# The router's logits of a mixture of experts: token tiles or router weights as the array's stationary side

## The chip, the cores and the metric

The kernel runs on one core of one Trainium2 chip. The metric is the device time of one execution in microseconds (us). The program is a transformer of four blocks; the change touches only the last one, the mixture of experts, which takes the last 275 us or so of the span.

## The reference, cut to what matters

There are 4096 tokens of width 256. The last block takes the layer-normalised stream `x` and computes

```python
scores = jax.nn.sigmoid(x @ gate_W) * route_scale            # gate_W: 256 x 8, eight experts
topk_scores, topk_idx = jax.lax.top_k(scores, 2)
topk_w = topk_scores / topk_scores.sum(-1, keepdims=True)
gate_full = jnp.einsum('bsk,bske->bse', topk_w, onehot)      # onehot of topk_idx
h = jax.nn.gelu(jnp.einsum('bsd,edh->bseh', x, W1) + b1, approximate=False)
y = jnp.einsum('bseh,ehd->bsed', h, W2) + b2
expert_out = jnp.einsum('bse,bsed->bsd', gate_full, y)
shared = jax.nn.gelu(x @ Ws1 + bs1, approximate=False) @ Ws2 + bs2
return expert_out + shared
```

and the stream gets the layer norm of the result added. All arithmetic is in float32. The hidden width is 128.

## The kernel before, in words

`phase_experts` works on 8 supertiles `i` of 512 tokens (`NT` = 4 tiles of 128). Per supertile there are 9 steps `k`: step 0 is the shared expert, steps 1 to 8 are the experts. The running number is `c = 9i + k`. Each engine has its own program; they meet at semaphores, and each engine works strictly in the order that is written.

- **TensorE**, step `k`: `hidden(i, k)` (six matmuls of 512 columns, L1651, for the three products of high and low parts), then inserted work for the next supertile, then `outputs(c - 3)` (twelve matmuls of 256 columns, L1670; four more, L1665, for the biases at `k` = 0). The inserted work in supertiles 1 to 6 is: at `k` = 0 the eight transposes `turn_in(i + 1)` (L172) of the normalised tokens into `psT` and `psG`; at `k` = 2 `logits(i + 1)` (L1631); at `k` = 6 `turn_gates(i + 1)` (L1638, four transposes). In supertile 0 these stand at `k` = 3, 5 and 8. `psG` is one PSUM bank: it is used for half of the turned tokens, then for the logits, then for the turned gates.
- **`logits`** before: for each of 4 token tiles and 2 halves of the width, the 128 x 128 turned tokens are the stationary side and the router's 128 x 8 weights move. A plain float32 matmul shows in the trace as two pairs of weight load and matmul, so the 8 of them are 16 pairs. The result has tokens in the partitions and 4 x 8 columns.
- **ScalarE**, step `k`: `gelu(i, k)` (L1741), then `high(c - 1)` (L1752, the rounded high part of the gated hidden values), then at `k` = 3 `sigmoid(i + 1)` (L1724, with a table load ahead of it and another ahead of the next gelu), at `k` = 4 `shift_x` (L1757), at `k` = 7 `take_gates(i + 1)` (L1732 and L1733). `take_turned` copies stand at `k` = 0. In supertile 0 the sigmoid stands at `k` = 5.
- **VectorE**, step `k` of 1 to 8: `gate(i, k)` (L1541: hidden values times the gate broadcast; the first waits for the DMA of the gates), at `k` = 2 `take_y` and the statistics of the supertile before, at `k` = 3 `route_tokens(i + 1)` (L1501 to L1525: 24 small instructions in a chain), at `k` = 4 the statistics of supertile `i + 2` (L134 to L141), at `k` = 5 `add_y` (L1565), at `k` = 6 `normalize_x(i + 2)` (L148). In supertile 0 the routing stands at `k` = 5.
- **GpSimd**, step `k`: `low(c)` (L1801, the low part, h minus its high part), and the inverse roots of the layer norms (L161).
- **SyncE** issues the DMAs. `gates_out` writes the 8 rows of gates to memory and reads them back spread over all partitions (`gb`, 2 MB).

The work for the next supertile's gates thus runs: `turn_in`, `take_turned`, `logits`, `sigmoid`, `route_tokens`, `turn_gates`, `take_gates`, `gates_out`, and then the first `gate` of the next supertile.

Column tiles occur elsewhere in this kernel: attention's products with the values (L1008) put a 128 x 32 weight block into each of four column tiles, and 256 columns move.

Of the kernel before, what the change touches and what calls it, by code (L numbers as in the profile page):

```python
# [17 lines left out]
ACT = mybir.ActivationFunctionType  # L18
AX = mybir.AxisListType

P = 128
# [1336 lines left out]
def phase_experts(nc, x, gate_w, w1, b1_cols, w2, b2, ws1, bs1_col, ws2, bs2, route_scale, ident_d, gate_rows, x_out):  # L1358
# [8 lines left out]
    with ExitStack() as ctx:  # L1367
# [3 lines left out]
        wg = m.sb("wg", [P, KD, NE])  # L1371
# [19 lines left out]
        sig, score, pick, sel1, sel2 = (m.sb(s, [P, NT, NE]) for s in ("sig", "score", "pick", "sel1", "sel2"))  # L1391
# [8 lines left out]
        psX = (psT, psG)  # L1400
        ident_in, const_in, w_in, x_in = m.sem("ident_in"), m.sem("const_in"), m.sems("w_in", 2), m.sems("x_in", 4)
# [3 lines left out]
        logits_done, sig_ready, route, gates_ready = m.sem("logits_done"), m.sem("sig_ready"), m.sem("route"), m.sem("gates_ready")  # L1405
        g_turned, gT_ready, g_out, gb_in = m.sem("g_turned"), m.sem("gT_ready"), m.sem("g_out"), m.sems("gb_in", 2)
# [12 lines left out]
        def _(sp):  # L1419
# [23 lines left out]
            sp.dma_start(wg[:, :, :], gate_w.rearrange("(k p) e -> p k e", p=P)).then_inc(const_in, 16)  # L1443
# [24 lines left out]
        def _(dve):  # L1468
# [29 lines left out]
            def route_tokens(i):  # L1498
                r.start(i)
                dve.wait_ge(sig_ready, i + 1)  # L1500
                nc.vector.tensor_scalar(score[:, :, :], sig[:, :, :], r_scale[:, 0:1], None,  # L1501
# [72 lines left out]

            nc.vector.memset(b_e[:, :], 0.0).then_inc(b_set, 1)
# [17 lines left out]
            for i in range(NST):  # L1593
                if 0 < i < NST - 1:
                    take_turned(i + 1)
                for k in range(1, E):
# [6 lines left out]
                    if k == (5 if i == 0 else 3) and i + 1 < NST:  # L1603
                        route_tokens(i + 1)
# [11 lines left out]
        def _(pe):  # L1616
# [10 lines left out]
            def logits(i):  # L1627
                pe.wait_ge(xlo_ready, KD * (i + 1))
                for n in range(NT):
                    for k in range(KD):  # L1630
                        mm = pe.matmul(psG[:, n * NE:(n + 1) * NE], xT[:, k, n * P:(n + 1) * P], wg[:, k, :],  # L1631
                                       start=(k == 0), stop=(k == KD - 1))
                mm.then_inc(logits_done, 1)

# [45 lines left out]
            for k in range(3):  # L1680
                hidden(0, k)
            turn_gates(0)

            for i in range(NST):
                for k in range(E):
# [3 lines left out]
                    if i + 1 < NST:  # L1689
# [9 lines left out]
                        if k == (8 if i == 0 else 6):  # L1699
                            turn_gates(i + 1)  # L1700
# [8 lines left out]
        def _(act):  # L1709
# [10 lines left out]
            def sigmoid(i):  # L1720
                act.wait_ge(logits_done, i + 1)
                if i:
                    act.wait_ge(gates_ready, i)
                nc.scalar.activation(sig[:, :, :], psG[:, 0:NT * NE].rearrange("p (n e) -> p n e", e=NE),  # L1724
                                     ACT.Sigmoid).then_inc(sig_ready, 1)
# [1104 lines left out]
```

## Time and profile before

| | us |
|---|---|
| time, median of 3 runs (lowest, highest) | 2087.64 (2087.29, 2089.38) |
| the profiled execution's own time | 2088.27 |
| its span | 2086.1 |
| TensorE matmul busy in the span | 1990.2 (95%) |
| VectorE busy | 1513.8 (73%) |
| ScalarE busy | 1288.2 (62%) |
| GpSimd busy | 599.2 (29%) |

All times in the profile count from the span's start. The experts' block begins at about 1812 us. Of an engine, "busy" is the time in which it executes an instruction; matmuls overlap, so that the duration of one is longer than the distance from one to the next. The numbers behind `x` count instructions.

### The profile page before, as it was taken

The numbers are of one execution on the slowest core, as the hardware profiler recorded it, in microseconds if no ns is written. First come the engines' busy times: TensorE is split into PE (matmuls) and PEld (weight loads), VectorE is DVE, ScalarE is ACT, GpSimd is POOL, SyncE is SP. The second block draws the span as 40 slices with busy tenths as digits, with TensorE's granted clock in tenths as the row PEclk, the third lists the DMA queues.
The fourth block names the chain that finished last, engine by engine and source line by source line (L and its number), as shares of the span: only waits on it lengthen the run. The fifth ranks groups of instructions, "written<-read, shape, count | busy, mean of one in ns | idle before, by whom it ended". The sixth has DMA issues, their size and how long they took to land. (4 is left out here: it accounts for less than half of the span.)

```text
span 2086.1 us, 42106 instructions
## 1 busy us (share of the span) xinstructions
PE 1990.2 (95%) x16914; PEld 1405.2 (67%) x16914; DVE 1513.8 (73%) x2466; ACT 1288.2 (62%) x2560; POOL 599.2 (29%) x480
## 2 busy tenths in 40 slices
PE   7999999999999998997999999999999999489997
PEld 6743333333333347986888888888888888478996
DVE  7889999999999976895546464646464644468774
ACT  3258888888888876785454545454545454256663
POOL 1200000000000014554334343434343433125554
PEclk9979999999999999999999999999999999789999
DMA  6832232223223222316222122212122212232221
GB/s 231 249 59 66 54 85 61 64 69 70 71 53 84 66 76 67 128 41 173 72 63 92 63 92 63 92 63 92 63 92 63 92 63 82 62 120 77 107 112 71
DMA packets 103490, 180.66 MB, mean 87 GB/s; under 512 B 24232, under 2 KB 65856, under 8 KB 98176
## 3 DMA queue, kind: packets, MB, share of 16 engines
q1 hardware_dynamic: 103296, 177.97, 28.4%
q8 instruction: 134, 2.20, 0.5%
q14 instruction: 60, 0.49, 0.1%
HBM read 138.48 MB, written 38.67 MB: 85 GB/s over the span
## 5 line engine op out<-in xcount | busy, mean ns | idle before, releaser
L741 DVE TENSOR_REDUCE att_sb_mx<-att_ps_psM 128x1 f32<-128x1024 f32 x512 | 624.6, 1221 | 27.6 <-PE att_ps_psM L978 23.8
L1192 ACT ACTIVATE att_sb_pt<-att_ps_psSO 128x512 f32<-128x512 f32 x1024 | 557.1, 597 | 95.2 <-PE att_ps_psSO L996 41.1
L978 PE MATMUL att_ps_psM<-stack_sb_k,stack_sb_q 48*128 48x512 f32 x1024 | 382.3, 454 | 4.6 <-DVE att_sb_mx L741 2.3
L996 PE MATMUL att_ps_psSO<-stack_sb_q,stack_sb_k 50*128 50x512 f32 x1024 | 373.3, 444 | 0.9 <-DMA stack_sb_q<-att_sb_mrow 0.9
L1008 PE MATMUL att_ps_psSO<-att_sb_pt,stack_sb_v 128*32 128x256 f32 x4096 | 326.4, 391 | 8.6 <-ACT att_sb_osb L1185 8.6
L996 PEld LDWEIGHTS att_ps_psSO<-stack_sb_q,stack_sb_k 50*128 50x128 f32 x1024 | 153.2, 185 | 202.8 <-ACT att_sb_pt L1192 155.5
L1008 PEld LDWEIGHTS att_ps_psSO<-att_sb_pt,stack_sb_v 128*32 128x32 f32 x4096 | 82.0, 108 | 192.1 <-issue 102.9
L2310 ACT ACTIVATE glag_sb_sg<-att_ps_psM 128x512 f32<-128x512 f32 x64 | 38.3, 599 | 250.9 <-PE att_ps_psM L2070 250.8
L2535 DVE TENSOR_TENSOR glaj_sb_dm<-att_ps_psSO,glaj_sb_dm 128x512 f32<-128x512 f32 x128 | 82.2, 684 | 133.5 <-PE att_ps_psSO L2190 133.5
L978 PEld LDWEIGHTS att_ps_psM<-stack_sb_k,stack_sb_q 48*128 48x128 f32 x1024 | 156.9, 189 | 19.3 <-DVE att_sb_mx L741 16.4
L2672 POOL TENSOR_TENSOR glaj_sb_dm<-glaj_sb_dm,glaa_sb_masked 128x1024 f32<-128x1024 f32 x64 | 156.5, 2466 | 19.0 <-DMA glaj_sb_dm<-decay_rows 19.0
L2327 ACT ACTIVATE glaj_sb_dm<-glaj_sb_dm,glaa_sb_neg_g 128x128 f32<-128x128 f32 x512 | 156.3, 391 | 0.2
L1801 POOL TENSOR_TENSOR moe_sb_hlo<-moe_sb_h,moe_sb_hhi 128x512 fp32r<-128x512 f32 x72 | 94.9, 1330 | 101.6 <-ACT moe_sb_hhi L1752 101.6
L2107 PE MATMUL att_ps_psM<-glao_sb_wo,glai_sb_yT 128*128 128x256 f32 x512 | 117.5, 382 | 0.9 <-DVE glai_sb_yT L2550 0.9
L1278 POOL TENSOR_TENSOR att_sb_mparts<-att_sb_mx,att_sb_zero 128x16 fp32r<-128x16 f32 x32 | 7.0, 220 | 383.8 <-DVE att_sb_mx L741 383.8
L1287 POOL TENSOR_TENSOR att_sb_on<-att_sb_osb,att_sb_rb 128x512 f32<-128x512 f32 x32 | 41.0, 1282 | 221.9 <-DMA att_sb_rb<-sums 221.9
L2107 PEld LDWEIGHTS att_ps_psM<-glao_sb_wo,glai_sb_yT 128*128 128x128 f32 x512 | 94.8, 190 | 13.8 <-DVE glai_sb_yT L2550 1.1
L2460 DVE SCALAR_TENSOR_TENSOR glah_sb_kg<-glag_sb_sg,att_ps_psM 128x512 f32<-128x512 f32 x64 | 44.0, 688 | 80.0 <-PE att_ps_psM L2070 65.7
L2680 POOL TENSOR_TENSOR glah_sb_kg<-glah_sb_kg,glaa_sb_to_end 128x1024 f32<-128x1024 f32 x32 | 65.0, 2032 | 92.5 <-PE att_ps_psM L2141 92.5
L1670 PE MATMUL moe_ps_psY<-moe_sb_wb_hi,moe_sb_hhi 128*128 128x256 f32 x288 | 83.7, 291 | 2.7 <-POOL moe_sb_hlo L1801 2.7
L2699 POOL TENSOR_TENSOR glah_sb_state<-glah_sb_state,glai_sb_eg 128x512 f32<-128x512 f32 x32 | 34.0, 1063 | 181.2 <-PE att_ps_psSO L2205 181.2
L2588 DVE TENSOR_REDUCE glaa_sb_osum<-glai_sb_osq 128x128 f32<-128x1024 f32 x32 | 63.7, 1990 | 30.3 <-ACT glai_sb_osq L2390 30.1
(305 smaller groups left out, 4829.0 us busy)
## 6 DMA issues: line engine op xcount, KB each, us to landing
glaj_sb_dm<-decay_rows SPq DMA_DIRECT2D x32, 1024.0 KB, 5.2
qk_parts<-stack_sb_part SPq DMA_DIRECT2D x32, 512.0 KB, 3.3
glai_sb_eg<-decay_exp SPq DMA_DIRECT2D x64, 256.0 KB, 6.3
moe_sb_gb<-gate_rows SPq DMA_DIRECT2D x8, 2048.0 KB, 7.7
stack_sb_q<-qk_parts SPq DMA_DIRECT2D x192, 64.0 KB, 3.0
stack_sb_k<-qk_parts SPq DMA_DIRECT2D x96, 128.0 KB, 4.3
att_sb_rb<-sums SPq DMA_DIRECT2D x32, 256.0 KB
attended<-att_sb_on SPq DMA_DIRECT2D x32, 256.0 KB, 4.9
```

What stands on the lines that cost most here:

```text
L741: nc.vector.tensor_reduce(mx[:, qh, 8 * r + c:8 * r + c + 1], psM[:, t % 2, :], AX.X, ALU.max).then_inc(maxima_taken, 1)
L978: mm = pe.matmul(psM[:, t % 2, c * ST:(c + 1) * ST], q[rs, g, qh, j, n * P:(n + 1) * P], k[rs, g, j, c * ST:(c + 1) * ST], start=True, sto ...
L996: pe.matmul(psS[:, ring_slot(pos), :], k[rs, g, j, s * P:(s + 1) * P], q[rs, g, qh, j, :], start=True, stop=True).then_inc(ring_done, 1)
L1008: mm = pe.matmul(psO[VW * j:VW * (j + 1), cols], v[:, KT * b + s, h:h + VW], pt[:, s % (LAG + 2), j, cols], start=(s == 0 and part == 0), ...
L1192: nc.scalar.activation(pt[:, s % (LAG + 2), ORDER[i], :], psS[:, (pos + 1) % 3, :], ACT.Exp, scale=AD ** -0.5).then_inc(ring_taken, 1)
L1670: mm = pe.matmul(psY[:, i % 2, n, :], v[:, c % 4, cols], w[:, e, :], start=False, stop=(k == E - 1 and p == 2), skip_group_check=True)
L1801: nc.gpsimd.tensor_tensor(hlo[:, c % 4, :], h[:, c % 4, :], hhi[:, c % 4, :], ALU.subtract).then_inc(hlo_ready, 1)
L2107: pe.matmul(psW[:, 0:D], yT[:, j, :], wo[:, j, :], start=(j == 0), stop=(j == J - 1))
L2327: done = nc.scalar.activation(dm[n % 2][:, h, :], dm[n % 2][:, h, :], ACT.Exp, bias=neg_g[:, u, n, h:h + 1])
L2535: nc.vector.tensor_tensor(dm[n % 2][:, hs, :], psA[:, odd, :, :], dm[n % 2][:, hs, :], ALU.mult).then_inc(ad_ready, 1)
L2672: nc.gpsimd.tensor_tensor(dm[n % 2][:, hs, :], dm[n % 2][:, hs, :], masked[:, :].rearrange("p (h t) -> p h t", h=1).to_broadcast([P, 8, P] ...
L2680: nc.gpsimd.tensor_tensor(kg[:, n % 2, :].rearrange("p (h d) -> p h d", d=GD), kg[:, n % 2, :].rearrange("p (h d) -> p h d", d=GD), to_end ...
```

## The change

The stationary and the moving side of the logits change places. The router's weights, padded from 8 to 32 columns with zeros, are the stationary side, and the 128 tokens of a tile move. The result of token tile `n` goes to partitions `32n` to `32n + 32` (a column tile of the array each), 128 columns wide: experts in the partitions, tokens in the columns. ScalarE takes the sigmoid of the whole 128 x 128 block into `sigT`; TensorE turns `sigT` back (`turn_scores`) into the second quarter of `psG`, and `route_tokens` reads the scores from there. `wg` is set to zero by VectorE before its DMA, and SyncE waits for that.

The positions move too: on VectorE `route_tokens(i + 1)` goes from step 3 to step 4 (5 to 6 in supertile 0), behind `gate(i, 4)`; on TensorE `turn_scores(i + 1)` stands at step 4 (6 in supertile 0) and `turn_gates(i + 1)` goes from step 6 to step 7 (it stays at 8 in supertile 0). In the prologue, `turn_scores(0)` follows `hidden(0, 0)`.

```diff
-        wg = m.sb("wg", [P, KD, NE])
+        wg, sigT = m.sb("wg", [P, KD, 32]), m.sb("sigT", [P, P])
...
+        psSig = psG[:, P:2 * P].rearrange("p (n e) -> p n e", e=32)
...
-            sp.dma_start(wg[:, :, :], gate_w.rearrange("(k p) e -> p k e", p=P)).then_inc(const_in, 16)
+            sp.wait_ge(wg_clear, 1)
+            sp.dma_start(wg[:, :, 0:NE], gate_w.rearrange("(k p) e -> p k e", p=P)).then_inc(const_in, 16)
...
             def route_tokens(i):
-                dve.wait_ge(sig_ready, i + 1)
-                nc.vector.tensor_scalar(score[:, :, :], sig[:, :, :], r_scale[:, 0:1], None,
+                dve.wait_ge(sig_turned, i + 1)
+                nc.vector.tensor_scalar(score[:, :, :], psSig[:, :, 0:NE], r_scale[:, 0:1], None,
...
+            nc.vector.memset(wg[:, :, :], 0.0).then_inc(wg_clear, 1)
...
-                    if k == (5 if i == 0 else 3) and i + 1 < NST:
+                    if k == (6 if i == 0 else 4) and i + 1 < NST:
                         route_tokens(i + 1)
...
             def logits(i):
                 pe.wait_ge(xlo_ready, KD * (i + 1))
-                for n in range(NT):
-                    for k in range(KD):
-                        mm = pe.matmul(psG[:, n * NE:(n + 1) * NE], xT[:, k, n * P:(n + 1) * P], wg[:, k, :],
+                for k in range(KD):
+                    for n in range(NT):
+                        mm = pe.matmul(psG[32 * n:32 * (n + 1), 0:P], wg[:, k, :], xT[:, k, n * P:(n + 1) * P],
                                        start=(k == 0), stop=(k == KD - 1))
                 mm.then_inc(logits_done, 1)
+
+            def turn_scores(i):
+                pe.wait_ge(sig_ready, i + 1)
+                pe.transpose(psG[:, P:2 * P], sigT[:, :], ident[:, :]).then_inc(sig_turned, 1)
...
-            for k in range(3):
+            hidden(0, 0)
+            turn_scores(0)
+            for k in (1, 2):
                 hidden(0, k)
...
-                        if k == (8 if i == 0 else 6):
+                        if k == (6 if i == 0 else 4):
+                            turn_scores(i + 1)
+                        if k == (8 if i == 0 else 7):
                             turn_gates(i + 1)
...
             def sigmoid(i):
                 act.wait_ge(logits_done, i + 1)
                 if i:
-                    act.wait_ge(gates_ready, i)
-                nc.scalar.activation(sig[:, :, :], psG[:, 0:NT * NE].rearrange("p (n e) -> p n e", e=NE),
-                                     ACT.Sigmoid).then_inc(sig_ready, 1)
+                    act.wait_ge(sig_turned, i)
+                nc.scalar.activation(sigT[:, :], psG[:, 0:P], ACT.Sigmoid).then_inc(sig_ready, 1)
```

## Rows read from the trace of the kernel before

**Rows 1.** Busy us (and count) per engine by window, TensorE clock, DMA share, GB/s.
```profile
1877.09:1907.85 30.76, 29.43 (x196) 26.37 (x195) 23.27 (x64) 18.88 (x32) 15.28 (x13) 1.00 0.28 105
...
1907.85:1936.98 29.13, 29.13 (x197) 26.47 (x195) 21.21 (x62) 17.73 (x30) 14.33 (x12) 1.00 0.29 110
...
sum 148.22, PE 146.04 PEld 132.24 DVE 110.93 ACT 92.31 POOL 74.52; mean PE 29.21 PEld 26.45 DVE 22.19 ACT 18.46 POOL 14.90
```

**Rows 2.** Waits of TensorE in 1800 to 2087: us in total, times, longest.
```profile
PE moe_ps_psG L1638 <- DVE moe_sb_gparts L1525: 1.6, 3, 0.8
```

**Rows 3.** The chain of waits: start, us, what.
```profile
1825.98 3.56 PE moe_ps_psG L1631 x16
...
1903.40 1.39 PE moe_ps_psH L1651 x6
...
1904.79 1.69 PE moe_ps_psG L1631 x16
...
1927.95 8.27 DMA moe_sb_gb<-gate_rows
```

**Rows 4.** Timeline of TensorE in attention: start, us, instruction, count.
```profile
400.95 0.39 PE L978 MATMUL att_ps_psM<-stack_sb_k,stack_sb_q 48*128 48x512 f32 x1
...
401.27 0.64 PE L1008 MATMUL att_ps_psSO<-att_sb_pt,stack_sb_v 128*32 128x256 f32 x8
...
401.84 0.28 PE L1016 MATMUL att_ps_psSO<-att_sb_ident,att_sb_mparts 128*32 128x128 f32 x1
```

**Rows 5.** Timeline of TensorE in supertile 2 of the experts.
```profile
1927.24 0.60 PE L172 MATMUL moe_ps_psT<-moe_sb_ident,moe_sb_xn 128*128 128x128 f32 x4
...
1928.03 0.36 PE L1670 MATMUL moe_ps_psY<-moe_sb_wb_hi,moe_sb_hhi 128*128 128x256 f32 x1
```

**Rows 6.** Timeline of ScalarE in supertile 2, and one line's durations (min/median/max).
```profile
1909.45 0.69 ACT L1741 ACTIVATE moe_sb_h<-moe_ps_psH,moe_sb_b_h 128x512 f32<-128x512 f32 x1 [2.19 <-PE moe_ps_psH L1651]
...
1910.66 1.28 ACT L1724 ACT_TABLE_LOAD   x1
...
1911.96 0.20 ACT L1724 ACTIVATE moe_sb_sig<-moe_ps_psG 128x32 f32<-128x32 f32 x1
...
1913.47 0.69 ACT L1741 ACTIVATE moe_sb_h<-moe_ps_psH,moe_sb_b_h 128x512 f32<-128x512 f32 x1
...
L2327 ACT ACTIVATE glaj_sb_dm<-glaj_sb_dm,glaa_sb_neg_g x512: 384/391/414, 976.6 to 1780.1; 128x128 f32<-128x128 f32 x171
```

**Rows 7.** Timeline of VectorE in supertile 2.
```profile
1911.31 0.68 DVE L1541 TENSOR_TENSOR moe_sb_h<-moe_sb_h,moe_sb_gb 128x512 f32<-128x512 f32 x1
...
1912.19 0.24 DVE L1501 TENSOR_SCALAR moe_sb_score<-moe_sb_sig,moe_sb_r_scale 128x32 f32<-128x32 f32 x1 [0.19 <-ACT moe_sb_sig L1724]
...
1913.36 1.11 DVE L1495 TENSOR_TENSOR moe_sb_sel<-moe_sb_pick,moe_sb_rank 128x32 f32<-128x32 f32 x1
...
1918.15 0.68 DVE L1541 TENSOR_TENSOR moe_sb_h<-moe_sb_h,moe_sb_gb 128x512 f32<-128x512 f32 x1
...
1920.81 0.68 DVE L1541 TENSOR_TENSOR moe_sb_h<-moe_sb_h,moe_sb_gb 128x512 f32<-128x512 f32 x1
...
1924.03 0.68 DVE L1541 TENSOR_TENSOR moe_sb_h<-moe_sb_h,moe_sb_gb 128x512 f32<-128x512 f32 x1
...
1924.64 2.35 DVE L148 TENSOR_SCALAR moe_sb_xn<-moe_sb_xin,moe_sb_mv,moe_sb_rs 128x256 f32<-128x256 f32 x4
```

**Rows 8.** Timeline of GpSimd in supertile 2.
```profile
1913.12 1.29 POOL L1801 TENSOR_TENSOR moe_sb_hlo<-moe_sb_h,moe_sb_hhi 128x512 fp32r<-128x512 f32 x1
```

**Rows 9.** Timeline of supertile 0: ScalarE, VectorE, TensorE.
```profile
1857.76 0.69 ACT L1741 ACTIVATE moe_sb_h<-moe_ps_psH,moe_sb_b_h 128x512 f32<-128x512 f32 x1
...
1862.38 0.68 DVE L1541 TENSOR_TENSOR moe_sb_h<-moe_sb_h,moe_sb_gb 128x512 f32<-128x512 f32 x1
...
1862.80 0.60 PE L1638 MATMUL moe_ps_psG<-moe_sb_ident,moe_sb_gparts 128*104 128x128 f32 x4
...
1867.72 0.66 PE L172 MATMUL moe_ps_psG<-moe_sb_ident,moe_sb_xn 128*128 128x128 f32 x4 [1.07 <-ACT moe_sb_gT L1733]
```

More of the change, by code:

```diff
@@ L1390, in phase_experts @@
         y, xo = m.sb("y", [P, NT, D]), m.sb("xo", [P, 2, NT, D])
-        sig, score, pick, sel1, sel2 = (m.sb(s, [P, NT, NE]) for s in ("sig", "score", "pick", "sel1", "sel2"))
+        score, pick, sel1, sel2 = (m.sb(s, [P, NT, NE]) for s in ("score", "pick", "sel1", "sel2"))
         gates, gT = m.sb("gates", [P, NT, NE]), m.sb("gT", [NE, 2, ST])
@@ L1405, in phase_experts @@
         logits_done, sig_ready, route, gates_ready = m.sem("logits_done"), m.sem("sig_ready"), m.sem("route"), m.sem("gates_ready")
+        sig_turned, wg_clear = m.sem("sig_turned"), m.sem("wg_clear")
         g_turned, gT_ready, g_out, gb_in = m.sem("g_turned"), m.sem("gT_ready"), m.sem("g_out"), m.sems("gb_in", 2)
```

## The prediction, made before the changed kernel was run

> **What bounds the kernel now.** I read the busy time by window first, one window from the third `hidden` step of a supertile to that of the next (the start of `hidden(i, 3)`, which I call P; in supertile 2 P is 1907.85, where the second window shown begins [rows 1]). The reader is to see that TensorE has 29.13 us of work in a window of 29.13 us, at the full clock, 146.04 of 148.22 us over five windows, while VectorE has 22.19 and ScalarE 18.46 on average [rows 1]. So TensorE sets the pace. The waits come next: what little TensorE waits for in the steady part is mostly VectorE's gate parts, 3 times and 1.6 us in all [rows 2]. VectorE's chain is therefore only just early enough. The chain of waits shows the same: it goes over the logits in one supertile and over the 8.27 us DMA of the gates in the next [rows 3]. The timelines last: I measure every event of supertile 2 from P and ask how much room each has.
>
> **The logits.** Removed: 16 pairs in 1.69 us, once in each of supertiles 0 to 6, and once in the prologue, in 3.56 us [rows 3]. Added: 8 float32 matmuls with 32 stationary and 128 moving columns. The nearest rows are attention's: four such matmuls of 256 columns, 8 records, take 0.57 us from their start at 401.27 to the next instruction at 401.84, and the first starts 0.32 us behind the 512-column matmul ahead of it [rows 4], where such a matmul takes 0.23 us in a row of its kind (1.39 us for six [rows 3]). So the four tiles run beside each other, two passes of 256 columns cost 0.48 us, and entering and leaving the column tiles costs some 0.09 us each. Here there are two k halves of two passes, each of 128 columns: four rounds of about 0.12 us, plus 0.2 us, 0.7 us. Bounds: 0.5 us (four rounds of 0.11 us and free changes of mode) and 1.9 us (16 passes of 0.11 us that don't overlap, with both changes). I take 0.7, since [rows 4] show the same weight shape and the same rotation over four tiles.
>
> The Trainium skill has a rule against column tiles, in the page TensorEngine Tiling (Array Packing), section Tiling Modes: changing the mode drains the array. By the trace that drain is the 0.09 us on either side, so it is in the sum; nothing else hangs on the rule.
>
> **Turning the scores back.** One transpose. Eight transposes fill 1927.24 to 1928.03 [rows 5], 0.10 us each; I take 0.13, between 0.10 and 0.30 for one that is alone. TensorE's own work per supertile falls by 1.69 - 0.70 - 0.13 = 0.86 us, to 28.3 us. Does it wait for the sigmoid? The sigmoid ends at P + 4.31 (1912.16) before [rows 6]. `hidden(4)` starts at P + 3.31 and is through at P + 4.70. A sigmoid of 128 x 128 instead of 128 x 32 takes 0.20 us at the least and 0.39 at the most, the 128 x 128 activation of line 2327 [rows 6]; I take 0.28, from the line between 0.20 us for 32 columns and 0.69 for 512. It ends at P + 4.4, 0.3 us ahead of need. No wait.
>
> **Routing behind gate 4.** This is the costly part. Before: gate 3 ran at P + 3.46, and VectorE then routed from P + 4.34 to P + 10.30, while ScalarE loaded the gelu table and did gelu 4. Gate 4 came at P + 10.30, then statistics, gate 5 at P + 12.96, gate 6 at P + 16.18 and the normalised tokens from P + 16.79 to P + 19.14 [rows 7]. TensorE turned those at P + 19.39 [rows 5]: 0.25 us of room. After: gate 4 stands ahead of the routing, and gate 4 needs gelu 4, which ScalarE ends at P + 6.31 (1914.16) since two table loads of 1.28 us lie around the sigmoid [rows 6]; with the longer sigmoid P + 6.4. So VectorE stands idle for about 1.2 us and starts to route at P + 7.05, not P + 4.34. The 24 instructions take 5.96 us of which two were stretched to about 1 us by GpSimd's `low` (the selection at 1913.36 took 1.11 us and ended with the `low` that began at 1913.12 [rows 7, 8]); without such a stretch they take 4.4. In the new place `low(3)` and `low(4)` fall on them, so I keep 5.95. They end at P + 13.0. Gate 4 is no longer behind them, so statistics follow, gate 5 starts at P + 15.0 (2.1 us later than before), and the tokens are ready at P + 21.2. From the turn to the next P TensorE took 29.13 - 19.39 = 9.74 us, now 8.75. The period is 21.25 + 8.75 = 30.0 us. It was 29.13. TensorE's 0.86 us turn into waits, at `outputs(5)` first and then at the transposes.
>
> Bounds of the routing's length: 4.4 us (GpSimd never beside it) and 6.9 us (three `low` beside it). In every other supertile the gates' DMA takes 8.3 us instead of about 7 and the statistics of y come later, so that `low(2)`, `low(3)` and `low(4)` all lie on the routing: I add 0.7 us there, a period of 30.7 us. The SBUF - State Buffer page of the Trainium skill, section Who interferes with whom, says that a VectorE instruction with two SBUF inputs and a GpSimd instruction that reads SBUF lock each other out. By that rule the stretch goes wherever `low` goes and changes no number here.
>
> **Turning the gates at step 7.** The gate parts are ready at P + 13.0, and TensorE comes there at P + 13.4; before both were at P + 10.4. No wait, and `take_gates` (ScalarE, step 7) waits for `high(6)` behind gate 6 as before. The gates' DMA keeps 0.8 us of room: gate 6 at P + 18.2, then 12.3 us to the landing (gate 6 at 1924.03, landing 1936.3, from the 8.27 us DMA issued at 1927.95 [rows 3, 7]), P + 30.5; two gates, y and its statistics and gate 3 take 5.1 us, P + 35.6, and gelu 4 of the next supertile comes at 36.4 or later.
>
> **Supertile 0 and the prologue.** Logits in the prologue save some 2 us of 3.56 [rows 3], but the scores wait for `hidden(0, 0)`, at half clock, and VectorE routes 1.5 us later: the two about cancel (bounds -1 and +1.5). In supertile 0 gate 6 moves ahead of the routing and waits for gelu 6, which starts at 1857.76 [rows 9]; routing runs from 1859.1 to 1864.9, not to 1862.47, and TensorE, which turned gates at 1862.80 without a wait, stands 2.1 us. VectorE then wins back one stretch: the turned gates reach ScalarE 0.95 us late, and TensorE's second half of the turned tokens, at 1867.72 before, comes 1 us late, which the faster logits of supertile 1 give back. P of supertile 2 is unchanged at 1907.85.
>
> **The small edits.** The memset of `wg`, some 0.1 us, runs when VectorE has nothing to do before its first tokens land, and SyncE reaches its wait four DMAs later: 0 (0.1 if it isn't covered).
>
> **The sum.** From P of supertile 2 to P of supertile 6 it was 148.22 - 30.76 = 117.46 us (the first window is 30.76) [rows 1]. After: 30.0 + 30.7 + 30.0 + 30.7 = 121.4, +3.9. In supertile 6 gate 5 comes 2.1 us later against P, and `add_y` behind it has one `low` fewer on it, -1.0: gate 6, and with it the last DMA of gates, is 5.0 us late. Supertile 7 hangs on that DMA (VectorE waits for it, then TensorE), so the end is 5.0 us late. The profiled execution took 2088.27 (span 2086.1 and 2.2 around it): 2093.2. That one lies 0.6 above the median of the runs, so I predict 2092.6 against 2087.64: slower by 0.24%.
>
> **The rivals.**
> (A) TensorE stays the bound. The routing meets only one or no `low` in its new place: 4.4 us, tokens ready at P + 19.7, then the period is 28.5 and for each of the six supertiles 0.8 us are won, one or two in the prologue lost: 2083. For it: TensorE is full in [rows 1]. Against it: `low(3)` follows gelu 4 by 0.6 us, so at least it lies at the routing's start; the change needs both `low` away.
> (B) Half of that: one stretch gone, or the 0.25 us of room larger than it seems; a period of 29.2 to 29.5, the same as before: 2086 to 2089.
> (C) The column tiles don't overlap for 128 columns, or their weight loads can't be hidden: logits of 1.7 to 1.9 us. 1.1 us more in each of five periods: 2098. This is also the case where the change doesn't do what it says. Against it: eight column-tile records in 0.57 us [rows 4].
> (D) The forecast's mechanism with routing slower still (three stretches everywhere): 2095.
>
> **How the numbers follow.** The forecast's own case has 0.50, with a range of 2090 to 2096; B 0.22; A 0.14; C 0.07; D 0.07. A measurement of this kernel tells about 0.2% (4.2 us) from nothing, so the bounds are 2083.5 and 2091.8. The forecast lies close to the upper one: a quarter of its chance falls below. Faster is A, 0.14; same is B and 0.12 of the forecast, 0.34; slower the rest, 0.52. The range reaches down to most of B and a part of A, up to C: 2084.5 to 2098.
>
> **What the changed profile would show.** The logits in 0.6 to 0.8 us (right) or over 1.5 (C). VectorE idle ahead of gate 4, released by gelu 4, about 1 us in supertiles 2, 4 and 6; the routing from P + 7. TensorE waiting for the normalised tokens at line 172 and for `low` at the outputs, 1 to 2 us in each supertile, where it waited for neither. In supertile 0 a wait of 2 us for the gate parts. If those waits are absent and TensorE is full in windows of 28.3 us, the forecast is wrong and A holds; if the waits stand there and the sum is smaller, the routing's length is the term that is off.

## The result, and the profile after

The changed kernel took 2094.73 us (median of 10 runs, 2092.85 to 2099.82), the kernel before 2087.47 (10 runs, 2086.65 to 2090.52): a ratio of 1.0035, 95% interval 1.0026 to 1.0043. It is slower by some 7 us; the forecast was slower by 5. The profiled execution of the changed kernel has a span of 2095.2 us, 9.1 more than before. 1.0 of that lies ahead of the experts' block, where nothing was changed (the block began at 1812.48 us and now at 1813.49), and 8.1 in the block, which took 273.64 us and now 281.69. The block's start lies anywhere from 1811.8 to 1817.0 us in the profiles of this page, though nothing ahead of it differs, so I compare the length of the block from here on.

The windows of the changed kernel, from the third `hidden` step of a supertile (P) to the next, columns as in [rows 1]:

```profile
1878.93:1911.12 32.19, 29.11 (x197) 24.70 (x196) 23.35 (x64) 18.43 (x31) 15.21 (x12) 1.00 0.30 109
1911.12:1941.06 29.94, 28.52 (x197) 24.89 (x196) 21.04 (x62) 18.43 (x31) 15.14 (x12) 1.00 0.28 106
1941.06:1972.29 31.23, 28.91 (x197) 24.72 (x196) 23.44 (x64) 18.43 (x31) 15.21 (x12) 1.00 0.27 103
...
sum 153.67, PE 143.82 PEld 124.12 DVE 111.63 ACT 92.21 POOL 75.70; mean PE 28.76 PEld 24.82 DVE 22.33 ACT 18.44 POOL 15.14
```

TensorE is busy for 2.2 us less in the five windows (143.82 for 146.04), and the windows are 5.5 us longer (153.67 for 148.22 [rows 1]). (Some 4.5 us of work were taken from it in them, as shown below; the matmuls beside a wait are spread, which hides a part of that.) It is no longer the engine that is full. The waits of TensorE from 1800 us to the end (total, times, longest), in the changed kernel, to be held against [rows 2]:

```profile
PE moe_ps_psY L1679 <- POOL moe_sb_hlo L1813: 11.1, 9, 1.7
...
PE moe_ps_psG L1647 <- DVE moe_sb_gparts L1529: 2.2, 2, 2.0
...
PE moe_ps_psG L1642 <- ACT moe_sb_sigT L1737: 0.8, 1, 0.8
```

The kernel before has the first of them too, but small:

```profile
PE moe_ps_psY L1670 <- POOL moe_sb_hlo L1801: 2.7, 3, 1.1
```

Those three waits lie in supertiles 0, 1 and 7. Now there is one of 1.3 to 1.4 us in each of supertiles 1 to 5: TensorE stands at the output matmuls for GpSimd's `low`, which is late because the gate ahead of it is. The two other lines are the gate parts, nearly all of it in supertile 0, and one wait of the turn-back for the sigmoid. VectorE's wait for gelu, in the changed kernel and then before:

```profile
DVE moe_sb_h L1545 <- ACT moe_sb_h L1753: 21.1, 11, 3.1
```
```profile
DVE moe_sb_h L1541 <- ACT moe_sb_h L1741: 8.6, 4, 2.9
```

These are the 12 us that VectorE lost by the move: it had the routing to do while ScalarE loaded its tables, and now it waits. Supertile 2 shows it step by step (P is 1911.12). First TensorE:

```profile
1908.69 0.39 PE L1660 MATMUL moe_ps_psH<-moe_sb_xhi,moe_sb_wa_lo 128*128 128x512 f32 x1
1909.01 0.64 PE L1636 MATMUL moe_ps_psG<-moe_sb_xT,moe_sb_wg 128*32 128x128 f32 x16
1909.58 0.39 PE L1679 MATMUL moe_ps_psY<-moe_sb_wb_hi,moe_sb_hhi 128*128 128x256 f32 x1
1909.80 0.28 PE L1679 MATMUL moe_ps_psY<-moe_sb_wb_hi,moe_sb_hlo 128*128 128x256 f32 x1
...
1915.58 0.40 PE L1660 MATMUL moe_ps_psH<-moe_sb_xhi,moe_sb_wa_lo 128*128 128x512 f32 x1
1915.81 0.28 PE L1642 MATMUL moe_ps_psG<-moe_sb_ident,moe_sb_sigT 128*128 128x128 f32 x1
1915.85 0.36 PE L1679 MATMUL moe_ps_psY<-moe_sb_wb_hi,moe_sb_hhi 128*128 128x256 f32 x1
1916.05 0.29 PE L1679 MATMUL moe_ps_psY<-moe_sb_wb_hi,moe_sb_hlo 128*128 128x256 f32 x1
...
1929.13 0.39 PE L1679 MATMUL moe_ps_psY<-moe_sb_wb_hi,moe_sb_hhi 128*128 128x256 f32 x1 [1.34 <-POOL moe_sb_hlo L1813]
...
1932.29 0.66 PE L172 MATMUL moe_ps_psT<-moe_sb_ident,moe_sb_xn 128*128 128x128 f32 x4
```

And the kernel before, around its logits and then where nothing stands between `hidden` and the outputs:

```profile
1904.40 0.39 PE L1651 MATMUL moe_ps_psH<-moe_sb_xhi,moe_sb_wa_lo 128*128 128x512 f32 x1
1904.63 1.84 PE L1631 MATMUL moe_ps_psG<-moe_sb_wg,moe_sb_xT 128*128 128x8 f32 x16
...
1906.53 0.28 PE L1670 MATMUL moe_ps_psY<-moe_sb_wb_hi,moe_sb_hlo 128*128 128x256 f32 x1
...
1912.32 0.39 PE L1651 MATMUL moe_ps_psH<-moe_sb_xhi,moe_sb_wa_lo 128*128 128x512 f32 x1
...
1912.66 0.28 PE L1670 MATMUL moe_ps_psY<-moe_sb_wb_hi,moe_sb_hlo 128*128 128x256 f32 x1
```

What an insertion costs shows in the distance from the last matmul of `hidden` to the second of the outputs, since the instructions beside the insertion are spread too. With nothing between it is 0.34 us (1912.32 to 1912.66). With the old logits it is 2.13, with the new ones 1.11, with the turn-back 0.47. So the old logits cost 1.79 us, the new ones 0.77 and the turn-back 0.13: 0.9 us less in each supertile. They are given back in the wait at 1929.13. Then ScalarE, with the two table loads around the sigmoid, and gelu 4 last:

```profile
1913.92 1.28 ACT L1737 ACT_TABLE_LOAD   x1
1915.22 0.28 ACT L1737 ACTIVATE moe_sb_sigT<-moe_ps_psG 128x128 f32<-128x128 f32 x1
1915.51 1.28 ACT L1753 ACT_TABLE_LOAD   x1
1916.81 0.69 ACT L1753 ACTIVATE moe_sb_h<-moe_ps_psH,moe_sb_b_h 128x512 f32<-128x512 f32 x1
```

VectorE of the same supertile: gate 4, the scores, the two instructions of the routing that are stretched (they take 0.19 us elsewhere), its last one, and gates 5 and 6:

```profile
1917.53 1.06 DVE L1545 TENSOR_TENSOR moe_sb_h<-moe_sb_h,moe_sb_gb 128x512 f32<-128x512 f32 x1 [1.88 <-ACT moe_sb_h L1753]
1918.52 0.24 DVE L1505 TENSOR_SCALAR moe_sb_score<-moe_ps_psG,moe_sb_r_scale 128x32 f32<-128x32 f32 x1
...
1919.01 0.79 DVE L1493 TENSOR_TENSOR moe_sb_pick<-moe_sb_score,moe_sb_best 128x32 f32<-128x32 f32 x1
...
1921.18 0.95 DVE L1493 TENSOR_TENSOR moe_sb_pick<-moe_sb_score,moe_sb_best 128x32 f32<-128x32 f32 x1
...
1924.04 0.19 DVE L1529 TENSOR_TENSOR moe_sb_gparts<-moe_sb_gates,moe_sb_gparts 128x32 fp32r<-128x32 f32 x1
...
1926.08 0.69 DVE L1545 TENSOR_TENSOR moe_sb_h<-moe_sb_h,moe_sb_gb 128x512 f32<-128x512 f32 x1
...
1929.28 0.68 DVE L1545 TENSOR_TENSOR moe_sb_h<-moe_sb_h,moe_sb_gb 128x512 f32<-128x512 f32 x1
```

And GpSimd: two `low` end to end, then a third; both stretched instructions of the routing end within 0.05 us of one of them (1919.75 and 1922.09), and gate 4 (1917.53 to 1918.59) lies beside the end of the first and the start of the second, which takes 1.67 us in place of 1.3.

```profile
1916.75 3.00 POOL L1813 TENSOR_TENSOR moe_sb_hlo<-moe_sb_h,moe_sb_hhi 128x512 fp32r<-128x512 f32 x2
1920.78 1.31 POOL L1813 TENSOR_TENSOR moe_sb_hlo<-moe_sb_h,moe_sb_hhi 128x512 fp32r<-128x512 f32 x1 [1.03 <-ACT moe_sb_hhi L1764]
```

### The profile page after: what moved, and what is told of

Its sections match the earlier page's. It is cut to its first block and busy times, and to the rows that moved or that the text cites. A ratio compares the mean times of both kernels' runs of the same rounds, so it can differ in the third digit from the quotient of the medians.

```text
span 2095.2 us, 42123 instructions
## 1 busy us (share of the span) xinstructions
PE 1987.9 (95%) x16922; PEld 1395.5 (67%) x16922; DVE 1512.1 (72%) x2467; ACT 1289.0 (62%) x2560; POOL 601.0 (29%) x480
## 5 line engine op out<-in xcount | busy, mean ns | idle before, releaser
L2119 PE MATMUL att_ps_psM<-glao_sb_wo,glai_sb_yT 128*128 128x256 f32 x512 | 117.5, 382 | 0.9 <-DVE glai_sb_yT L2562 0.9
```

Of the source, the lines that this page charges most:

```text
L2119: pe.matmul(psW[:, 0:D], yT[:, j, :], wo[:, j, :], start=(j == 0), stop=(j == J - 1))
```

## The experiments

The theory is that of the forecast: a period is VectorE's part from P to the normalised tokens (gelu 4, gate 4, routing, statistics, gates 5 and 6) and then TensorE's part from the turned tokens to the next P, one behind the other. The rivals: the logits' new form itself costs something; TensorE sets the pace; or `low` is slow in itself, wherever it lies. The kernels of this section were run in five rounds against the kernel before, which had medians of 2088.8 to 2089.8 us beside them; where the changed kernel's time is compared with theirs, it is by the ratios to the kernel before, whose intervals are 0.0017 to 0.0027 wide (3.5 to 6 us). This table, worked out from the profiles, has the places at which the block can be compared; P(2) is P of supertile 2. The times are us; the last but one column is the DMA of the gates of supertile 7, from issue to landing.

| kernel | block's start to P(2) | P(2) to P(6) | P(6) to end | block | last gates' DMA | ratio (95%) |
|---|---|---|---|---|---|---|
| before | 95.4 | 117.5 | 60.8 | 273.6 | 8.44 | 1 |
| changed | 97.6 | 121.5 | 62.6 | 281.7 | 9.07 | 1.0035 (1.0026 to 1.0043) |
| tok_late | 98.1 | 126.6 | 62.4 | 287.2 | 8.64 | 1.0067 (1.0054 to 1.0081) |
| col_early | 95.0 | 116.3 | 61.5 | 272.9 | 8.31 | 0.9999 (0.9990 to 1.0008) |
| col_late_double | 99.1 | 123.7 | 61.6 | 284.5 | 8.17 | 1.0037 (1.0024 to 1.0050) |
| col_late_quad | 98.7 | 125.3 | 60.4 | 284.4 | 6.85 | 1.0050 (1.0037 to 1.0063) |
| col_late_sig2 | 97.4 | 121.5 | 60.9 | 279.8 | 7.57 | 1.0031 (1.0020 to 1.0041) |
| col_late_s0early | 96.3 | 124.1 | 62.5 | 282.9 | 9.02 | 1.0030 (1.0018 to 1.0042) |
| col_late_pro | 95.7 | 122.3 | 61.7 | 279.7 | 8.22 | 1.0032 (1.0020 to 1.0045) |
| col_late_smalllow | 95.3 | 115.7 | 61.2 | 272.2 | 9.13 | 0.9983 (0.9974 to 0.9992) |
| tok_smalllow | 94.9 | 115.9 | 59.6 | 270.4 | 8.74 | 0.9985 (0.9976 to 0.9994) |
| col_early_pro | 92.8 | 116.4 | 62.1 | 271.4 | 8.78 | 0.9985 (0.9977 to 0.9994) |
| col_best | 93.2 | 118.6 | 62.9 | 274.7 | 9.99 | 0.9999 (0.9990 to 1.0008) |
| col_best2 | 93.0 | 115.3 | 61.4 | 269.7 | 8.59 | 0.9981 (0.9973 to 0.9990) |

That column is there because in all 14 profiles the span ends 33.3 to 33.4 us behind the landing of this DMA, while the DMA itself takes from 6.85 to 9.99 us, with no order that I can tell. Two blocks of one profile each therefore differ by up to 3 us through this DMA alone; below I say where a difference comes from it.

**tok_late: the old logits, the new positions.** Against the kernel before:

```diff
-                    if k == (5 if i == 0 else 3) and i + 1 < NST:
+                    if k == (6 if i == 0 else 4) and i + 1 < NST:
                         route_tokens(i + 1)
...
-                        if k == (8 if i == 0 else 6):
+                        if k == (8 if i == 0 else 7):
                             turn_gates(i + 1)
```

> The kernel before with only the positions of the change: route_tokens one step later (step 4, behind gate 4; step 6 in supertile 0) and turn_gates at step 7. The logits stay in token tiles. My theory (the period is VectorE's part from P, the start of hidden(i, 3), to the turn of the tokens, plus TensorE's part from there to the next P) says that the late routing alone costs more than the whole change, since the TensorE part keeps its 1.69 us of logits: about 1 us a supertile above the changed kernel, less 1 to 2 us of prologue, 2098 to 2101 us. The rival (the column-tiled logits with their turn back are what costs, the order is harmless) says 2087 to 2089 us.

Measured: 2103.58 us, the slowest of all, 2.6 us over the top of my 2098 to 2101 (2 us of that are the slower kernel before beside it, 2089.79 us). TensorE has its old work back and waits as in the changed kernel (the windows' sum, then the waits):

```profile
sum 158.35, PE 148.52 PEld 131.33 DVE 113.70 ACT 92.29 POOL 75.25; mean PE 29.70 PEld 26.27 DVE 22.74 ACT 18.46 POOL 15.05
```
```profile
PE moe_ps_psY L1670 <- POOL moe_sb_hlo L1801: 10.7, 9, 1.7
PE moe_ps_psG L1638 <- DVE moe_sb_gparts L1525: 4.9, 6, 2.7
```

The late routing alone costs 13.5 us of block, and the column form then wins 5.5 of them (287.2 to 281.7). The loss is the move's, not the logits'.

**col_early: the new logits, the old positions of the routing.** Against the changed kernel:

```diff
-                    if k == (6 if i == 0 else 4) and i + 1 < NST:
+                    if k == (5 if i == 0 else 3) and i + 1 < NST:
                         route_tokens(i + 1)
```

> The changed kernel with route_tokens back at step 3 (5 in supertile 0), ahead of gate 4; turn_scores and turn_gates stay at steps 4 and 7. My theory: routing starts when the turned scores arrive, at P + 5.0 instead of P + 7.1, the tokens are ready at P + 19.8, the period is 28.6 to 29.1 us, and the whole 2084 to 2088 us. The rival (the column-tiled logits with their turn back are what costs) says 2093 to 2096 us, as the changed kernel.

Measured: 2089.06 us, no difference from before (ratio 0.9999, the upper end of what I had given). The sum of its windows:

```profile
sum 146.79, PE 144.38 PEld 124.49 DVE 110.28 ACT 91.91 POOL 73.82; mean PE 28.88 PEld 24.90 DVE 22.06 ACT 18.38 POOL 14.76
```

The block is 0.8 us shorter than before and 8.8 shorter than the changed one. So 0.9 us less TensorE work per supertile is worth about 0.1 with the routing at its old place: VectorE's chain, which had 0.25 us of room, takes over at once (TensorE waits for the normalised tokens by 0.08 us in each of supertiles 1 to 5, where it did not wait before). The turned scores also reach it at P + 5.0, where the sigmoid's reached it at P + 4.3.

**col_late_double and col_late_quad: the logits two and four times over.** Against the changed kernel (2, then 4; each time the sums start anew):

```diff
-                for k in range(KD):
+                for k in list(range(KD)) * (2 if i else 1):
                     for n in range(NT):
```

> The changed kernel with the logits of the loop computed twice (the second time over the first; the result is the same), 0.6 us more of TensorE per supertile. My theory says that TensorE's work between the turn of the tokens and P counts in full even though TensorE now waits 1 to 2 us elsewhere: 7 x 0.6 = 4 us more than the changed kernel, 2098 to 2100 us. The rival (TensorE has become slack, VectorE's chain alone sets the time) says 2094 to 2096 us.

Measured: 2097.9 us, which by its ratio isn't told from the changed kernel. The block grew by 2.8 us, near seven times 0.44. But the parts don't fit a cost per supertile: the periods from supertile 1 on grew by 1.4, 0.4, 0.3, 1.6, 0.0 and 0.0 us. The two large ones are those whose gates' DMA took longer here (9.81 us for 8.37 ahead of supertile 1, 8.63 for 7.07 ahead of supertile 4). So the dose was raised:

> The changed kernel with the eight logit matmuls of each supertile 1 to 7 issued four times over (each time they start their sums anew, so nothing else changes). Issued twice they took 1.08 us in place of 0.64 in the trace, so three more times cost 1.3 us, all of it between the turning of the tokens and the third hidden step. Theory (the period is VectorE's part from the third hidden step to the normalised tokens, plus TensorE's part from there on, which counts in full): each steady period 1.3 us longer, 31.2 and 32.5 in place of 29.9 and 31.2, seven times 1.3, +9 us, a ratio to the kernel before of about 1.0078. Rival (the column tiles' saving is off the path with late routing, the period hangs on VectorE, ScalarE and GpSimd alone, and TensorE has 1 to 2 us of waits to take it from): +0 to +3 us, a ratio of 1.0035 to 1.005.

Measured: 2100.01 us, block +2.7. Windows of supertiles 2 and 3:

```profile
1910.97:1942.19 31.22, 29.83 (x246) 26.22 (x245) 21.74 (x62) 18.42 (x31) 14.94 (x13) 1.00 0.28 102
1942.19:1973.40 31.21, 29.83 (x246) 26.24 (x244) 21.15 (x62) 17.79 (x30) 14.21 (x12) 1.00 0.28 103
```

The theory's +9 missed. The rival's 0 to +3 holds the number, and 2.2 us of what is missing lie in the last gates' DMA (6.85 us for 9.07), but the rival's reason is wrong too. Splitting each period at the turn of the tokens shows why. TensorE's part, from the turn to the next P, is 10.07 or 10.08 us in each of supertiles 1 to 5, where it was 8.77 or 8.78: the extra 1.3 us is paid each time. VectorE's part, from P to the turn, stays at 21.15 in supertile 2 (so this period grows by 1.28 us, from 29.94 to 31.22), and shrinks from 23.41 to 21.14 in supertile 1 and from 22.45 to 21.14 in supertile 3 (so that this one doesn't grow, 31.23 to 31.21).

In the changed kernel gate 1 of supertile 3 comes at P + 0.56, since its gates' DMA takes 8.32 us (8.37 for supertile 1, 6.99 to 7.26 for 0, 2, 4, 5 and 6) and lands late; `low(2)` then slips to P + 7.33, and three `low` lie on the routing (at P + 7.33, 8.56 and 10.28), which takes 7.16 us. With the logits at four times, gate 1 comes at P - 1.97, `low(2)` is done at P + 6.53 and the routing takes 6.07. Gate 4 comes 0.2 us sooner too. Of these 2.5 us of gate 1 one half is the later P; the other is a shorter DMA (7.10 us). The later P alone would do: supertile 4 of this kernel has a long DMA (8.36 us), gate 1 at P - 0.72, two `low` on its routing and a period of 31.22. So the sum of two parts holds, but VectorE's part isn't a constant: it hangs on when the gates land, measured from P.

**col_late_smalllow and tok_smalllow: the stretch taken away.** GpSimd's subtraction of steps 3 and 4 covers 8 of its 512 columns in supertiles 1 to 7, in the changed kernel and in the kernel before (the low parts of two experts' activations are left out):

```diff
-                nc.gpsimd.tensor_tensor(hlo[:, c % 4, :], h[:, c % 4, :], hhi[:, c % 4, :], ALU.subtract).then_inc(hlo_ready, 1)
+                some = slice(0, 8) if c > E and c % E in (3, 4) else slice(0, ST)
+                nc.gpsimd.tensor_tensor(hlo[:, c % 4, some], h[:, c % 4, some], hhi[:, c % 4, some], ALU.subtract).then_inc(hlo_ready, 1)
```

> The changed kernel in which GpSimd computes the low part of steps 3 and 4 only for 8 of 512 columns in supertiles 1 to 7 (it leaves out the rest of that part of the computation), so that next to nothing of GpSimd lies beside the routing. My theory: the two or three instructions of the routing that take about 1 us each go back to 0.2 us, the routing takes 4.4 to 4.8 us instead of 5.7 to 7.2, VectorE's part of the period shrinks by 1 to 2.5 us, and the period falls to 28.3 to 29 us: 2086 to 2089 us, about as the kernel before. The rival (the long instructions of the routing come from something else, such as the DMA or PSUM) leaves the routing at 6 us and the time at 2094 to 2096 us.

> The kernel before, with GpSimd's subtraction of steps 3 and 4 cut to 8 of its 512 columns in supertiles 1 to 7 (what it leaves out: the low parts of two experts' activations). Theory (with early routing TensorE sets the pace, and a routing that is stretched is hidden): the routing shortens from 6.0 to about 4.4 us, and the time falls by 3 us at most, the slack of the supertiles whose gates land late: periods of 29 us in all; ratio 0.9985 to 1.0. Rival (GpSimd's subtraction slows the kernel in general, not by lying on a late routing, so that the 10 us which the same edit took off the changed kernel come here too): -8 us or more, a ratio of 0.996 or below.

Measured: 2085.80 and 2085.13 us, ratios of 0.9983 and 0.9985; the first is a little below what I had given. The instructions that were stretched to 0.79 and 0.95 us in the changed kernel, in the first of the two:

```profile
1915.09 0.19 DVE L1493 TENSOR_TENSOR moe_sb_pick<-moe_sb_score,moe_sb_best 128x32 f32<-128x32 f32 x1
...
1916.66 0.19 DVE L1493 TENSOR_TENSOR moe_sb_pick<-moe_sb_score,moe_sb_best 128x32 f32<-128x32 f32 x1
```

Its routing takes 4.36 us in supertile 2 (the forecast gave 4.4 for no `low` beside it), and its periods are 28.7 and 29.3, though VectorE still waits for gelu 4 until P + 6.41. The same cut takes 9.5 us off the changed block and only 3.3 off the old one, whose supertile 2 then looks so, TensorE full:

```profile
1909.49:1938.46 28.97, 28.97 (x197) 26.54 (x195) 20.96 (x62) 18.48 (x31) 12.07 (x12) 1.00 0.30 110
```

(3.3 us of block is a little over the 3 that I had set as the most.) `low` therefore doesn't cost the same wherever it lies; 6.2 of the 8.1 us go with `low` lying on a routing that can no longer be hidden. (The cut also makes these two `low` ready a us sooner; that this isn't what counts is seen in supertile 2, where the routing is 1.36 us shorter and the period 1.2.) With it cut in both, the two kernels differ by 1.8, of which 1.6 lie behind P(6) (0.4 of them the last gates' DMA).

**col_late_sig2: the sigmoid one step earlier.** In the changed kernel:

```diff
-                    if i + 1 < NST and k == (5 if i == 0 else 3):
+                    if i + 1 < NST and k == (5 if i == 0 else 2):
                         sigmoid(i + 1)
```

> The changed kernel with ScalarE's sigmoid one step earlier in supertiles 1 to 6 (step 2, ahead of gelu 3, so that both table loads are over before gelu 4 is due); nothing else moves. My theory (gate 4, and with it the routing, waits for gelu 4 behind two table loads) says that gate 4 comes 0.8 us earlier against P and the whole is 4 to 5 us shorter than the changed kernel: 2089.5 to 2091.5 us. The rival (gate 4 is as late through VectorE's own queue, the table loads are off the path) says 2094 to 2096 us.

Measured: 2096.08 us, not told from the changed kernel; my 4 to 5 us did not come. The block is 1.9 us shorter, but 1.5 of that is the last gates' DMA (7.57 us for 9.07); P(2) to P(6) is the same. (Supertile 0 is 0.9 us longer than in the changed kernel; there the granted clock fell to 0.50 for 3.4 us, 1.3 us behind a wait of 1.99.) In supertile 2 gate 4 starts 0.8 us earlier against P (5.62), but now lies on two `low`: VectorE, then GpSimd:

```profile
1916.86 1.37 DVE L1545 TENSOR_TENSOR moe_sb_h<-moe_sb_h,moe_sb_gb 128x512 f32<-128x512 f32 x1 [0.68 <-ACT moe_sb_h L1753]
1918.15 0.24 DVE L1505 TENSOR_SCALAR moe_sb_score<-moe_ps_psG,moe_sb_r_scale 128x32 f32<-128x32 f32 x1
```
```profile
1916.38 3.00 POOL L1813 TENSOR_TENSOR moe_sb_hlo<-moe_sb_h,moe_sb_hhi 128x512 fp32r<-128x512 f32 x2
```

It took 1.37 us where alone it takes 0.68, and the scores are only 0.5 us earlier (P + 6.91). The wait for gelu and the stretch by `low` trade against each other.

**col_late_s0early: the routing of supertile 0 back at step 5.**

```diff
-                    if k == (6 if i == 0 else 4) and i + 1 < NST:
+                    if k == (5 if i == 0 else 4) and i + 1 < NST:
```

> The changed kernel with the routing of supertile 0 alone back at step 5, ahead of gate 6. My theory: TensorE's wait of 2 us for the gate parts in supertile 0 goes, the gates' DMA of supertile 1 lands about 1.5 us earlier, and with it all that follows: 1 to 1.5 us less than the changed kernel, 2093 to 2094 us; in the block the first two periods are 1.5 to 2.5 us shorter together. The rival (the first supertiles are slow through the prologue, the wait for gate parts is hidden by the later supertiles) says no difference, and first periods as in the changed kernel.

Measured: 2095.21 us, not told from the changed kernel. Supertile 0 takes 40.6 us for 41.2, as before the change (40.5); supertile 1 still 32.2. So the late routing of supertile 0 costs 0.65, not the 1.5 to 2.5 that I expected of the first two periods, and more is lost in supertile 1. (Here the gates' DMA of supertile 5 took 9.82 us, and that period 32.7; it is why this block isn't the shorter one.)

**col_late_pro and col_early_pro: the scores of the prologue turned back at once**, ahead of `hidden(0, 0)`, in the changed kernel and in col_early:

```diff
             logits(0)
+            turn_scores(0)
             pe.wait_ge(w_lo_ready, 1)
-            hidden(0, 0)
-            turn_scores(0)
-            for k in (1, 2):
+            for k in range(3):
                 hidden(0, k)
```

> The changed kernel with the prologue's turn_scores(0) right behind logits(0), ahead of hidden(0, 0). The scores are turned while TensorE waits for the low weights anyway, so routing starts 3.5 us earlier and the tokens of supertile 1 are turned up to 3.5 us earlier. My theory: up to P of supertile 1 it is 0.5 to 1.5 us shorter (the gates' DMA of supertile 0 is the next limit), the whole 2093 to 2094.5 us. The rival (supertile 0 hides the prologue) says 2094.5 to 2095.5 us.

> Column tiles with routing at step 3 (5 in supertile 0), as in the run col_early, and turn_scores(0) right behind logits(0) in the prologue. My theory: what the prologue gives stands beside what the early routing gives: 0.5 to 1.5 us less than col_early, at 0.9995 of the kernel before. The rival says as col_early.

Measured: 2096.04 and 2087.02 us. The first P comes 1.4 to 1.5 us earlier in both. Behind the late routing 0.5 of it is left at the next P. There TensorE waited 2.67 us for the gate parts of supertile 0, and 0.6 us behind that wait its granted clock fell from 1.00 to 0.50 for 3.4 us, in which its output matmuls came 0.21 us apart for 0.12. The block is 2.0 us shorter (0.85 of it the last gates' DMA), and the time isn't told from the changed kernel's. Behind the early one 2.5 us are won at the next P and 1.5 in the block, and that kernel is faster than the kernel before (0.9985); that it is faster than col_early isn't certain, since their intervals overlap. TensorE waits for the low half of the weights before `hidden(0, 0)` in any case (1.3 us in the changed kernel; here 0.39 for the sigmoid and 0.43 for the weights), so the sigmoid is covered.

**col_best and col_best2: all of it with early routing.** col_best is col_early_pro with the sigmoid and `turn_scores` one step earlier (2 and 3), the gates still turned at 7. In col_best2 the sigmoid stands right behind gelu 2, ahead of `high(1)`, and the gates are turned at 6. Of the second, against the first:

```diff
                         gelu(i, k)
+                    if i and i + 1 < NST and k == 2:
+                        sigmoid(i + 1)
...
-                    if i + 1 < NST and k == (5 if i == 0 else 2):
+                    if i == 0 and k == 5:
                         sigmoid(i + 1)
```

> Column tiles with everything pulled forward: sigmoid at step 2, turn_scores at step 3, routing at step 3 (ahead of gate 4), turn_gates at step 7, and turn_scores(0) right behind logits(0). My theory: the scores lie turned in PSUM when VectorE comes to them, the routing starts right behind gate 3 (P + 4.2 to P + 5.5), the tokens are ready at P + 19 to P + 20.5, and the period is 28.3 to 29.2 us instead of 29.4: 2083 to 2086 us, 0.998 to 0.999 of the kernel before. The rival (with VectorE's chain and the gates' DMA at 28.8 us as the next limit, nothing is won) says 0.9995 to 1.0005.

> As col_best, but the sigmoid of supertiles 1 to 6 stands right behind gelu 2, ahead of the high part that waits for the first gate. My theory of col_best's failure (ScalarE reached the sigmoid only after that high part, which waits for the gates' DMA, and TensorE stood at turn_scores for it) says that the waits of TensorE there, 8.2 us in col_best, go to under 2 us, the routing starts at P + 4.1 to P + 5, and the period is 28.4 to 29.0 us: 0.997 to 0.9985 of the kernel before, and not slower than col_early_pro. The rival (the gates' DMA and VectorE's chain are the limit whatever ScalarE does) says as col_early_pro, 0.998 to 0.999.

Measured: 2089.63 and 2086.47 us. In col_best TensorE waits for the sigmoid, which stands behind `high(1)` and so behind gate 1 and the gates' DMA:

```profile
PE moe_ps_psG L1642 <- ACT moe_sb_sigT L1736: 8.2, 7, 2.9
```

Behind one of these waits, in supertile 3, the granted clock was 0.50 for 3.4 us, and that period is 31.78 us.

In col_best2 that wait is 0.6 us in all. Its supertiles 2 and 3:

```profile
1906.02:1934.31 28.29, 28.28 (x198) 25.04 (x196) 21.12 (x61) 18.44 (x32) 14.80 (x12) 1.00 0.31 111
1934.31:1964.19 29.88, 28.51 (x197) 24.93 (x196) 22.80 (x64) 18.63 (x32) 14.76 (x12) 1.00 0.28 108
```

28.29 us with TensorE full: here the column logits bring their 0.84 us against [rows 1]. The next supertile, with the long DMA of the gates, gives most of it back. This is the shortest block of all, 4.0 us under before; by time (0.9981) it beats both kernels, but the runs don't tell it from col_early_pro.

## Why the prediction was right

| step | forecast | measured |
|---|---|---|
| logits on TensorE | 0.7 us | 0.77 |
| turn-back | 0.13, no wait | 0.13; once 0.75 waited (supertile 1) |
| gelu 4 done, gate 4 starts | P + 6.4 | P + 6.41 |
| routing starts | P + 7.05 | P + 7.40 |
| routing, supertile 2 | 5.95 us | 5.72 |
| gate 5 | P + 15.0 | P + 14.96 |
| tokens turned | P + 21.25 | P + 21.17 |
| from there to the next P | 8.75 | 8.77 |
| periods 2 to 5 | 30.0, 30.7, 30.0, 30.7 | 29.94, 31.23, 29.93, 30.38 |
| P(2) to P(6) | 121.4 | 121.5 |
| wait of TensorE for the gate parts, supertile 0 | 2.1 us | 1.98 |
| P(2) against before | 0 | +2.3 |
| behind P(6), against before | +1.1 | +1.8 |

The mechanism was right and is shown from several sides: tok_late and col_early put the loss on the move, the two kernels with small `low` put 6.2 of 8.1 us on the stretched routing, and col_late_quad shows that TensorE's part counts in full. The routing began 0.35 us later than I had it, because gate 4 itself was stretched to 1.06 us by a `low`; the routing was 0.2 shorter, so that gate 5 stood where I had put it. (The trace has 22 instructions in the routing, not the 24 that I counted; its length was read off as a whole, so nothing changes.) The SBUF — State Buffer page of the Trainium skill, section Who interferes with whom, calls the port that VectorE and GpSimd share an exclusive lock; the trace agrees: instructions of 0.19 us in the routing took 0.78 to 1.28 and ended within 0.05 us of the `low`.

The terms that were mis-sized:
- The logits, a little: 0.77 us for 0.7. I had given the change of mode 0.09 us on either side, from attention; beside the 0.44 us that a further set costs there are 0.33 left.
- "P of supertile 2 is unchanged": it came 2.3 us late, 0.8 of it at P of supertile 1 and 1.4 in the period from there (32.19 for 30.76). I had seen the 2.1 us wait in supertile 0 and let the faster logits of supertile 1 pay it back. They couldn't: from supertile 1 on the period hangs on VectorE, and supertile 1 is one of those with the long DMA of the gates (gate 1 at P + 1.51, routing of 7.17 us). It should have been given the +0.7 and the wait of its period like supertile 3. Three `low` lie on its routing in the trace; in col_late_smalllow this period is 30.2. TensorE's granted clock isn't the cause: it was 0.50 for 10.2 us in supertile 0 where it had been so for 3.4, but gate 4 came at P + 16.45, as before (16.49).
- The slow supertiles: 31.23 for 30.7 in supertile 3. I had one more `low` at +0.7; the routing took 7.16 us, 1.2 over the forecast's 5.95 and over my upper bound of 6.9. Supertile 5, whose gates' DMA took only 7.26 us (8.48 before), had 30.38. That P(2) to P(6) came out at 121.5 for 121.4 is in part luck: one of the slow periods was 0.5 too long and the other 0.3 too short.
- TensorE waits at the outputs only. I had named the outputs first and the transposes behind; the latter waited 0.09 us or less, for the outputs' wait had already moved them.
- The end: 1.8 us behind P(6), of which I had 1.1. Gate 6 of supertile 6 came 1.11 us later against P, and the last gates' DMA was issued 1.10 later, as forecast. The rest is that DMA itself, which took 0.63 us longer, before and then after (start, us, what):

```profile
2044.37 8.44 DMA moe_sb_gb<-gate_rows
```
```profile
2052.76 9.07 DMA moe_sb_gb<-gate_rows
```

From its landing to the end it is 33.3 us before and 33.4 after. No run shows that the change makes this DMA longer.

Together 2.3 + 4.0 + 1.8 = 8.1 us, the block's growth. Rival A (TensorE stays the bound) and B fell with the windows, which have 143.82 us of work in 153.67. C fell with the logits at 0.77 us. D had 2095 us, nearer to the measured 2094.7 than my 2092.6; but its reason, three stretches everywhere, is true of supertiles 1 and 3 only, and that its number fits is luck.

What stays open: why the gates' DMA takes about 7 us one time and 8.4 another, on which the lengths of the periods hang. From issue to landing it was 7.21, 8.45, 7.01, 8.27, 6.94, 8.48, 6.99 and 8.44 us for supertiles 0 to 7 before, and 7.17, 8.37, 7.15, 8.32, 7.07, 7.26, 6.99 and 9.07 after. That looks like a change in turn, but col_late_quad has four short ones first (7.10 to 7.29), then 8.36 and 8.62.

## What to carry to other kernels

When an engine's chain is nearly as long as the busiest engine's work, moving one of its parts behind a wait costs nearly the whole wait (in supertile 2 VectorE waited 1.88 us ahead of gate 4, and the tokens were turned 1.79 us later against P), and freeing the busiest engine brings next to nothing: measure the room of the second chain (0.25 us here) before a saving is counted (TensorE had 0.9 us less to do in each of seven supertiles, and col_early's block is 0.8 us shorter in all). Price a moved VectorE chain with the GpSimd instructions that will lie on its new place, and with those that lie there when a transfer is late; here that was most of the loss. A column-tile form was worth having here, by 0.2% at best, but its turn-back needs the activation ahead of anything that waits for a DMA, and its prologue turn belongs directly behind the prologue's logits.

## What the runs showed of the hardware

- Eight float32 matmuls in four column tiles, 128 moving columns each (16 records), cost TensorE 0.77 us between full-array matmuls at a granted clock of 1.00; a second set adds 0.44 us (1.08 against 0.64 in the records), three more add 1.32 (1.96). A full-array matmul of 512 columns takes 0.23 us in a row of its kind, so 16 passes of 128 columns one behind the other would take 0.9 us: the tiles run beside each other. Of the 0.77 us, 0.33 remain beside the 0.44 of a set; they hold the changes between the modes, and no run takes them apart.
- One float32 transpose between other matmuls costs 0.13 us. From its start to the next instruction's it is only 0.04, but the instruction behind then takes 0.20 to its successor in place of 0.12: an insertion has to be measured over its neighbours.
- VectorE instructions of only 128 x 32 elements are held by a GpSimd instruction as long as large ones are, to its end: a chain of 22 small ones took 4.36 us with no `low` beside it, 5.1 to 5.3 with one, 5.7 to 6.5 with two and 7.0 to 7.2 with three. The reductions among them were never held. GpSimd pays too: two `low` took 3.00 us beside gate 4, where one takes 1.29.
- Within 1.3 us of the end of a wait of 2 to 2.7 us TensorE's granted clock fell from 1.00 to 0.50 for 3.4 us in three kernels (col_late_pro, col_late_sig2, col_best). It did not behind waits as long in the changed kernel (1.98 us), tok_late (2.7) and col_best (2.94).
